# A recurrent kernel whose doubled cell moves from SBUF into the PSUM bank of its tanh

## The chip, the cores and the metric

The kernel runs on one core of one Trainium2 chip. A core has TensorE (PE, matmuls), VectorE (DVE), ScalarE (ACT), GpSimd (POOL) and SyncE (SP, which issues DMAs), each with a queue of its own that is worked off in order; they meet by semaphores. SBUF is the working memory, PSUM the memory of eight banks that matmuls write. The metric is the device time of one execution in microseconds, lower is better.

## The reference

The block has three layers over x of 16 batches x 1024 steps x 64 features: a token mixing (q, k, v, scores times a gamma matrix, output and PReLU), a recurrent autoencoder on its layernorm (LSTMs of 128 units), and a mixture of 8 experts, two chosen for each token, on the layernorm of the sum. The recurrent part is this, cut:

```
def step(carry, xw):
    h, c = carry
    z = xw + h @ U
    i, f, g, o = jnp.split(z, 4, axis=-1)
    i = jax.nn.sigmoid(i)
    f = jax.nn.sigmoid(f)
    g = jnp.tanh(g)
    o = jax.nn.sigmoid(o)
    c = f * c + i * g
    h = o * jnp.tanh(c)
    return ((h, c), h)
...
h_fwd = _lstm(x @ Wf + bf, Uf, reverse=False)
h_bwd = _lstm(x @ Wb + bb, Ub, reverse=True)
latent = jnp.concatenate([h_fwd, h_bwd], axis=-1)
rep = jnp.broadcast_to(latent[:, None, :], (x.shape[0], x.shape[1], 2 * H))
dec = _lstm(rep @ Wd + bd, Ud, return_sequences=True)
return dec @ Wo + bo
```

The two LSTMs of the encoder and the one of the decoder take 1024 steps each, one step after the other.

## The kernel before

Four stages run one behind the other: the setup of weights, the token mixing, the encoder and the decoder. The diff touches the last two.

A `Chain` is one LSTM: fwd and bwd in the encoder, dec in the decoder. Everything is held transposed, 128 units on the partitions and 16 batches in a row, so a step works on tiles of 128x16. A sigmoid is computed as a tanh of half the argument: sigmoid(z) = (tanh(z/2) + 1)/2. A step of a chain is:

- PE, `pe_gates`: 12 matmuls of 128x16 into the PSUM banks of the gates; eight with the high half of the hidden state (`h_hi`, f16; L740, weights `u_lo` and `u_hi`), four with its low half (`h_lo`; L743). The parts from x and the bias are already there (`fill`).
- ACT, `act_gates`: one tanh of the gates i, f, g (L751, 128x48, to `ifg_cell`), one of o (L753).
- DVE, `dve_terms` (L766): (tanh + 1) times its partner, for two pairs at once: i with g, f with the old cell, which lies in `ifg_cell[:, 3]`. `dve_sum` (L772) adds the two: twice the new cell, `twice_cell`, in SBUF.
- ACT, `act_cell` (L758): tanh of half of `twice_cell`, written to the start of a PSUM bank (6 for fwd, 7 for bwd, 3 for dec).
- DVE or ACT, the output gate from tanh_o: in the encoder ACT (L777), in the decoder DVE (L789).
- DVE, `dve_hidden`: the hidden state as f16, called hi below (L797), and again as f32, called h (L798); `dve_hidden_low` (L803): the difference, called lo. PE waits for hi and for lo.
- DVE, `dve_half_cell` (L783): half of `twice_cell` back to `ifg_cell[:, 3]`, for the next step's terms.

The order on each engine is written out by hand. In the encoder the two chains alternate, each pass of `for d in range(2)` being a half-step: DVE does hi and h of the other chain (`late`), terms of chain d, lo of the late chain, sum and halving of chain d. ACT does tanh of the cell, the gates and the output gate of one chain, then of the other. PE does one chain's gates and then filler matmuls (`pe_idle`, L731: products that nobody reads, which keep PE busy) or the next `fill`.

In the decoder there is one chain, and tiles of 32 steps (`BODY`): while it goes through 32 steps, the experts and layernorms of the 32 steps before run beside it, cut into pieces and tied to a step. On DVE such a piece stands either behind the halving and ahead of hi (`in_tanh`, while ACT computes the tanh of the cell) or behind lo (`in_gates`). PE has the expert matmuls and, in steps 2 to 18, 10 or 13 fillers.

An instruction that reads what its own engine has just written waits for that by a semaphore too: the sum for the terms, lo for h, the halving for the sum.

Of the kernel before, what the change touches and what calls it, by code (L numbers as in the profile page):

```python
# [7 lines left out]
ALU = mybir.AluOpType  # L8
ACT = mybir.ActivationFunctionType
# [692 lines left out]
class Chain:  # L702
# [5 lines left out]

    def __init__(self, sb, sem, d, name, cell_bank):
        self.d = d  # L710
        self.tanh_cell = cell_bank[:, 0:B]
        self.ifg_cell = sb(f"ifg_cell_{name}", [P, 4, B], F32)
        self.terms = sb(f"terms_{name}", [P, 2, B], F32)
        self.twice_cell, self.tanh_o, self.out_gate, self.h = (
            sb(f"{part}_{name}", [P, B], F32) for part in ("twice_cell", "tanh_o", "out_gate", "h"))
        (self.s_z_ifg, self.s_z_o, self.s_t_ifg, self.s_t_o, self.s_terms, self.s_out_gate, self.s_twice,
         self.s_cell, self.s_tanh_cell, self.s_hi, self.s_h, self.s_lo) = (sem(f"{s}_{name}") for s in (
             "z_ifg", "z_o", "t_ifg", "t_o", "terms", "out_gate", "twice", "cell", "tanh_cell", "hi", "h", "lo"))

    def start(self, nc, own):  # L720

        own.link(nc.vector.memset(self.twice_cell[:], 0.0))
        nc.vector.memset(self.ifg_cell[:, 3, :], 0.0).then_inc(self.s_cell, 1)


# [29 lines left out]

def act_cell(nc, act, c, n):
    act.wait_ge(c.s_twice, n + 1)
    nc.scalar.activation(c.tanh_cell, c.twice_cell[:], ACT.Tanh, scale=0.5).then_inc(c.s_tanh_cell, 1)  # L758


def dve_terms(nc, dve, c, n, own_cell=True):
# [7 lines left out]

def dve_sum(nc, dve, c, n):  # L770
    dve.wait_ge(c.s_terms, n + 1)
    nc.vector.tensor_tensor(c.twice_cell[:], c.terms[:, 0, :], c.terms[:, 1, :], ALU.add).then_inc(c.s_twice, 1)  # L772


def act_out_gate(nc, act, c, n, half_scale):
# [3 lines left out]


def dve_half_cell(nc, dve, c, sums):
    dve.wait_ge(c.s_twice, sums)
    nc.vector.tensor_scalar(c.ifg_cell[:, 3, :], c.twice_cell[:], 0.5, None, ALU.mult).then_inc(c.s_cell, 1)  # L783


def dve_rest(nc, dve, c, n, sums):

    dve.wait_ge(c.s_t_o, n + 1)
    nc.vector.tensor_scalar(c.out_gate[:], c.tanh_o[:], 1.0, 0.5 * X_SCALE, ALU.add, ALU.mult  # L789
                            ).then_inc(c.s_out_gate, 1)  # L790
    dve_half_cell(nc, dve, c, sums)


def dve_hidden(nc, dve, c, n, h_hi):
# [11 lines left out]
def encoder(nc, m):  # L806

    ctx, sb, sem = tools(nc)
    with ctx:
        ch = [Chain(sb, sem, d, name, m.bank[6 + d]) for d, name in enumerate(("fwd", "bwd"))]
        s_set = sem("encoder_state_set")
        hello = sb("encoder_hello", [P, 1], F32)
        half_scale = sb("encoder_half_scale", [P, 1], F32)
        s_half_scale = sem("half_scale_set")
        h = list(zip(m.enc_hi, m.enc_lo))


        banks = [[ifg_bank(m, 2 * d + p) for p in range(2)] for d in range(2)]
        o_banks = [o_bank(m, 4 + d) for d in range(2)]

        def at(d, step):

            q, s = divmod(step, STEPS)
            s = STEPS - 1 - s if d else s
            return banks[d][q % 2][:, s], o_banks[d][:, s]

        with nc.Block() as block:
            @block.tensor
            def _(pe):
                def fill(d, q, k):

                    g = SLOT_GATE[k]
                    z = banks[d][q % 2][:, :, k, :] if k < 3 else o_banks[d]
                    z = z.rearrange("p t b -> p b t")
                    x = m.xs[:, CHUNKS - 1 - q if d else q, :, :]

                    nc.tensor.matmul(z, m.w_hi[d][:, g, :], x,  # L841
                                     start=(k in (0, 3)), stop=False, skip_group_check=True)
                    nc.tensor.matmul(z, m.w_lo[d][:, g, :], x,  # L843
                                     start=False, stop=False, skip_group_check=True)
                    nc.tensor.matmul(z, m.lstm_bias[d][:, GATE_FROM[g], :], m.ones3[:].rearrange("p (b t) -> p b t", b=B),  # L845
                                     start=False, stop=False, skip_group_check=True)

                for d in range(2):
                    for k in range(4):
                        fill(d, 0, k)  # L850
                for step in range(T):
                    q, s = divmod(step, STEPS)
                    for d in range(2):
                        pe_gates(nc, pe, m, ch[d], step, h[d][0][:], h[d][1][:], *at(d, step))
                        spare = m.bank[2 * d + 1 - q % 2][:, HALF - P:]
                        if s in (1, 3, 5) and q + 1 < CHUNKS:
                            fill(d, q + 1, s // 2)
                            pe_idle(nc, m, spare, 2)
                        elif s != (STEPS - 1 if d else 0):
                            pe_idle(nc, m, spare, 5)  # L860
                        else:
                            pe_idle(nc, m, spare, 2)
                        if d == 1 and s == STEPS - 1 and q + 1 < CHUNKS:
                            pe.wait_ge(ch[0].s_t_o, step + 1)
                            fill(0, q + 1, 3)
                        if d == 0 and s == 0 and q > 0:
                            pe.wait_ge(ch[1].s_t_o, step)
                            fill(1, q, 3)

            @block.scalar  # L870
            def _(act):
                nc.scalar.activation(hello[:], m.ident[:, 0:1], ACT.Gelu)
                act.wait_ge(s_half_scale, 1)
                for n in range(T):
                    act_cell(nc, act, ch[1], n)
                    act_gates(nc, act, ch[0], n, *at(0, n))
                    act_out_gate(nc, act, ch[0], n, half_scale[:])
                    act_cell(nc, act, ch[0], n)
                    act_gates(nc, act, ch[1], n, *at(1, n))
                    act_out_gate(nc, act, ch[1], n, half_scale[:])  # L880
                act_cell(nc, act, ch[1], T)

            @block.vector
            def _(dve):
                own = Links(dve, s_set)
                nc.vector.memset(half_scale[:], 0.5 * X_SCALE).then_inc(s_half_scale, 1)
                for d in range(2):
                    ch[d].start(nc, own)
                own.link(nc.vector.memset(ch[1].out_gate[:], 0.0))
                nc.vector.memset(h[0][0][:], 0.0).then_inc(ch[0].s_hi, 1)  # L890
                nc.vector.memset(h[0][1][:], 0.0).then_inc(ch[0].s_lo, 1)
                nc.vector.memset(ch[1].h[:], 0.0).then_inc(ch[1].s_twice, 1)

                def hidden(late, n):
                    dve.wait_ge(ch[late].s_tanh_cell, n + 1)
                    dve_hidden(nc, dve, ch[late], n, h[late][0][:])

                for n in range(T):
                    for d in range(2):

                        late = 1 - d
                        hidden(late, n)
                        dve_terms(nc, dve, ch[d], n, own_cell=False)
                        dve_hidden_low(nc, dve, ch[late], n, h[late][0][:], h[late][1][:])
                        dve_sum(nc, dve, ch[d], n)
                        dve_half_cell(nc, dve, ch[d], n + 1 + d)
                hidden(1, T)
                dve_hidden_low(nc, dve, ch[1], T, h[1][0][:], h[1][1][:])

# [8 lines left out]
def decoder_and_experts(nc, m):  # L918
# [7 lines left out]
    with ctx:  # L926
# [74 lines left out]
        with nc.Block() as block:  # L1001
# [199 lines left out]
            def _(dve):  # L1201
# [139 lines left out]
                def body(i, tiles):  # L1341
                    tiles = [(j, start, Own(dve, s_own, DVE_OWN * j)) for j, start in tiles]
                    for step in range(BODY):
                        n = BODY * i + step
                        dve_terms(nc, dve, c, n)
                        dve_sum(nc, dve, c, n)
                        dve_rest(nc, dve, c, n, n + 1)
                        part(in_tanh, tiles, step)
                        dve.wait_ge(c.s_tanh_cell, n + 1)
                        dve.wait_ge(c.s_out_gate, n + 1)  # L1350
                        dve_hidden(nc, dve, c, n, h_at(ring_hi, n))
                        dve_hidden_low(nc, dve, c, n, h_at(ring_hi, n), h_at(ring_lo, n))
                        part(in_gates, tiles, step)

# [29 lines left out]
```

## Time and profile before

| what | us |
|---|---|
| median of 3 runs | 3970.09 |
| lowest and highest | 3967.66 and 3974.99 |
| the profiled execution | 3965.94 |
| its span, first to last instruction | 3964.1 |
| busy: PE, DVE, ACT | 3694.0, 3134.2, 2392.3 |

The profile is one execution, recorded by the hardware. A row of a timeline has the start and duration of an instruction, and an instruction can start while the one ahead of it is still ending. The distance between the starts of two instructions is what a step is made of. The grouped rows give a mean duration in ns for each line, operation and shape.

### The profile page before, as it was taken

How to read it: one execution, taken by the hardware profiler on the slowest of the kernel's cores; microseconds unless marked ns; L12 is line 12 of the kernel's file. 1: busy time of each engine (PE TensorE's matmuls, PEld its weight loads, DVE VectorE, ACT ScalarE, POOL GpSimd, SP SyncE). 2: the span in 40 equal slices, each digit the busy share in tenths (PEclk: the TensorE clock that was granted, in tenths of full speed). 3: DMA queues.
4: the chain of work that ended last, by engine and by line, in shares of the span. 5: the costliest groups of instructions: out<-in, count | busy, mean ns of one | idle time of the engine just before them, and what ended most of it. 6: DMA issues, size and time to landing. Idle time of an engine off the chain costs nothing. (4 is left out here: it accounts for less than half of the span.)

```text
span 3964.1 us, 155805 instructions
## 1 busy us (share of the span) xinstructions
PE 3694.0 (93%) x59839; PEld 2626.1 (66%) x59839; DVE 3134.2 (79%) x21227; ACT 2392.3 (60%) x11882; POOL 85.2 (2%) x129
## 2 busy tenths in 40 slices
PE   6899899999999999999999798989999999999898
PEld 3233688888888888888887556555555555555564
DVE  5888899999999999999998667766666666666675
ACT  3222699999999999999987334344334443344443
POOL 6100000000000000000000000000000000000000
PEclk8999999999999999999999899999999999999999
DMA  3010000000000000000000000000000000000000
GB/s 90 20 24 20 7 3 3 3 3 3 3 3 3 3 3 3 3 3 3 3 3 4 5 6 7 8 6 7 6 8 8 6 6 7 7 7 7 6 7 7
DMA packets 49554, 33.73 MB, mean 9 GB/s; under 512 B 37661, under 2 KB 46877, under 8 KB 48806
## 3 DMA queue, kind: packets, MB, share of 16 engines
q1 hardware_dynamic: 48806, 23.77, 2.3%
q8 instruction: 468, 7.67, 0.8%
q14 instruction: 280, 2.29, 0.2%
HBM read 15.37 MB, written 8.39 MB: 6 GB/s over the span
## 5 line engine op out<-in xcount | busy, mean ns | idle before, releaser
L731 PE MATMUL bank<-xs,ident 128*128 128x128 f16 x13490 | 1209.0, 221 | 0.0
L731 PEld LDWEIGHTS bank<-xs,ident 128*128 128x128 f16 x13490 | 882.4, 102 | 60.5 <-issue 38.2
L751 ACT ACTIVATE ifg_cell_dec<-bank 128x48 f32<-128x48 f32 x1024 | 215.1, 210 | 664.7 <-PE bank L743 664.7
L766 DVE SCALAR_TENSOR_TENSOR terms_dec<-ifg_cell_dec 128x32 f32<-128x32 f32 x1024 | 196.5, 192 | 422.6 <-ACT ifg_cell_dec L751 411.7
L743 PE MATMUL bank<-enc_lo,u_hi 128*128 128x16 f16 x8192 | 529.2, 173 | 0.3 <-DVE enc_lo L803 0.3
L740 PE MATMUL bank<-enc_hi,u_lo 128*128 128x16 f16 x8192 | 527.0, 172 | 0.0
L740 PE MATMUL bank<-enc_hi,u_hi 128*128 128x16 f16 x8192 | 500.3, 169 | 0.0
L740 PEld LDWEIGHTS bank<-ring_hi,u_lo 128*128 128x128 f16 x4096 | 175.5, 97 | 485.1 <-DVE ring_hi L797 465.4
L740 PEld LDWEIGHTS bank<-enc_hi,u_lo 128*128 128x128 f16 x8192 | 338.8, 96 | 205.5 <-DVE enc_hi L797 171.4
L758 ACT ACTIVATE bank<-twice_cell_dec 128x16 f32<-128x16 f32 x1024 | 191.8, 187 | 401.9 <-DVE twice_cell_dec L772 401.9
L740 PE MATMUL bank<-ring_hi,u_lo 128*128 128x16 f16 x4096 | 264.2, 173 | 181.6 <-DVE ring_hi L797 148.4
L743 PEld LDWEIGHTS bank<-enc_lo,u_hi 128*128 128x128 f16 x8192 | 338.5, 96 | 67.5 <-DVE enc_lo L803 0.4
L740 PEld LDWEIGHTS bank<-enc_hi,u_hi 128*128 128x128 f16 x8192 | 349.6, 95 | 0.0
L777 ACT ACTIVATE out_gate_fwd<-tanh_o_fwd,encoder_half_scale 128x16 f32<-128x16 f32 x1024 | 315.2, 308 | 33.5
L777 ACT ACTIVATE out_gate_bwd<-tanh_o_bwd,encoder_half_scale 128x16 f32<-128x16 f32 x1024 | 314.9, 308 | 33.6
L843 PE MATMUL bank<-xs,w_lo 128*128 128x128 f16 x1024 | 322.4, 315 | 0.0
L845 PE MATMUL bank<-ones,bias 128*128 128x128 bf16 x1024 | 322.3, 315 | 0.0
L841 PE MATMUL bank<-xs,w_hi 128*128 128x128 f16 x1024 | 277.3, 271 | 1.4 <-PEq L432 1.4
L743 PE MATMUL bank<-ring_lo,u_hi 128*128 128x16 f16 x4096 | 263.2, 172 | 0.9 <-DVE ring_lo L803 0.9
L1112 PE MATMUL bank<-hid,w 128*64 128x512 f32 x448 | 258.1, 660 | 0.0
L740 PE MATMUL bank<-ring_hi,u_hi 128*128 128x16 f16 x4096 | 250.6, 169 | 0.0
L758 ACT ACTIVATE bank<-twice_cell_bwd 128x16 f32<-128x16 f32 x1025 | 192.0, 187 | 53.9
(268 smaller groups left out, 7900.4 us busy)
## 6 DMA issues: line engine op xcount, KB each, us to landing
g_rows<-tok_d_gamma_batched_dram SPq DMA_DIRECT2D x8, 512.0 KB, 6.5
x_rows<-in_x_dram SPq DMA_DIRECT2D x16, 256.0 KB, 3.1
kept_h<-tok_ln_h SPq DMA_DIRECT2D x32, 128.0 KB, 2.1
res<-kept_h SPq DMA_DIRECT2D x32, 128.0 KB
out_dram<-sums SPq DMA_DIRECT2D x32, 128.0 KB
raw_wd<-in_L_attn_Wd_dram SPq DMA_DIRECT2D x2, 256.0 KB
raw_experts<-in_L_ffn_W_dram SPq DMA_DIRECT2D x2, 256.0 KB
raw_u<-in_L_attn_Uf_dram SPq DMA_DIRECT2D x1, 256.0 KB
```

The lines of the kernel that those rows point to most:

```text
L731: nc.tensor.matmul(spare, m.ident16[:], m.xs[:, 0, :, :].rearrange("p b t -> p (b t)"), start=False, stop=True, skip_group_check=True)
L740: nc.tensor.matmul(z[k], w[:, g, :], h_hi, start=False, stop=False, skip_group_check=True)
L743: last = nc.tensor.matmul(z[k], m.u_hi[c.d][:, g, :], h_lo, start=False, stop=True, skip_group_check=True)
L751: nc.scalar.activation(c.ifg_cell[:, 0:3, :], ifg, ACT.Tanh, scale=1.0 / Z_SCALE).then_inc(c.s_t_ifg, 1)
L758: nc.scalar.activation(c.tanh_cell, c.twice_cell[:], ACT.Tanh, scale=0.5).then_inc(c.s_tanh_cell, 1)
L766: nc.vector.scalar_tensor_tensor(c.terms[:], c.ifg_cell[:, 0:2, :], 1.0, c.ifg_cell[:, 2:4, :], ALU.add, ALU.mult).then_inc(c.s_terms, 1)
L777: nc.scalar.activation(c.out_gate[:], c.tanh_o[:], ACT.Identity, scale=0.5 * X_SCALE, bias=half_scale).then_inc(c.s_out_gate, 1)
L841: nc.tensor.matmul(z, m.w_hi[d][:, g, :], x, start=(k in (0, 3)), stop=False, skip_group_check=True)
L843: nc.tensor.matmul(z, m.w_lo[d][:, g, :], x, start=False, stop=False, skip_group_check=True)
L845: nc.tensor.matmul(z, m.lstm_bias[d][:, GATE_FROM[g], :], m.ones3[:].rearrange("p (b t) -> p b t", b=B), start=False, stop=False, skip_gro ...
L1112: mm(y_bank[0:D, :], m.w2[:, e, :], hid[:, e % 2, :], start=False, stop=False, skip_group_check=True)
```

## The change

`twice_cell` no longer has an SBUF tile of its own. It is the second block of 16 columns in the chain's cell bank in PSUM, beside the tanh, so DVE's sum writes PSUM, and ACT's tanh and DVE's halving read it there. The halving, which stood beside the tanh, is moved behind it: in the decoder to between h and lo, in the encoder to half a step later, where it halves the late chain's cell. The terms of the encoder need it, and a wait for `s_cell` is added ahead of hi.

```diff
-        self.tanh_cell = cell_bank[:, 0:B]
+        self.tanh_cell, self.twice_cell = cell_bank[:, 0:B], cell_bank[:, B:2 * B]
...
 def dve_sum(nc, dve, c, n):
     dve.wait_ge(c.s_terms, n + 1)
-    nc.vector.tensor_tensor(c.twice_cell[:], c.terms[:, 0, :], c.terms[:, 1, :], ALU.add).then_inc(c.s_twice, 1)
+    nc.vector.tensor_tensor(c.twice_cell, c.terms[:, 0, :], c.terms[:, 1, :], ALU.add).then_inc(c.s_twice, 1)
...
 def dve_half_cell(nc, dve, c, sums):
     dve.wait_ge(c.s_twice, sums)
-    nc.vector.tensor_scalar(c.ifg_cell[:, 3, :], c.twice_cell[:], 0.5, None, ALU.mult).then_inc(c.s_cell, 1)
...
-def dve_rest(nc, dve, c, n, sums):
+    nc.vector.tensor_scalar(c.ifg_cell[:, 3, :], c.twice_cell, 0.5, None, ALU.mult).then_inc(c.s_cell, 1)
...
+def dve_out_gate(nc, dve, c, n):
...
-    dve_half_cell(nc, dve, c, sums)
...
                         late = 1 - d
+                        dve.wait_ge(ch[d].s_cell, n + 1 + d)
                         hidden(late, n)
                         dve_terms(nc, dve, ch[d], n, own_cell=False)
                         dve_hidden_low(nc, dve, ch[late], n, h[late][0][:], h[late][1][:])
                         dve_sum(nc, dve, ch[d], n)
-                        dve_half_cell(nc, dve, ch[d], n + 1 + d)
+                        dve_half_cell(nc, dve, ch[late], n + 1)
...
                         dve_sum(nc, dve, c, n)
-                        dve_rest(nc, dve, c, n, n + 1)
+                        dve_out_gate(nc, dve, c, n)
                         part(in_tanh, tiles, step)
                         dve.wait_ge(c.s_tanh_cell, n + 1)
                         dve.wait_ge(c.s_out_gate, n + 1)
                         dve_hidden(nc, dve, c, n, h_at(ring_hi, n))
+                        dve_half_cell(nc, dve, c, n + 1)
                         dve_hidden_low(nc, dve, c, n, h_at(ring_hi, n), h_at(ring_lo, n))
```

DVE's queue in the encoder, one half-step of the kernel before; in brackets the semaphores that an instruction waits for (`twice` is set by the sum, `cell` by the halving, `t_ifg` by ACT's tanh of the gates):

```order
L797 TENSOR_TENSOR enc_hi<-out_gate_bwd,bank 128x16 [waits tanh_cell_bwd]
L798 TENSOR_TENSOR h_bwd<-out_gate_bwd,bank 128x16
L766 SCALAR_TENSOR_TENSOR terms_fwd<-ifg_cell_fwd 128x32 [waits t_ifg_fwd]
L803 TENSOR_TENSOR enc_lo<-h_bwd,enc_hi 128x16 [waits h_bwd]
L772 TENSOR_TENSOR twice_cell_fwd<-terms_fwd 128x16 [waits terms_fwd]
L783 TENSOR_SCALAR ifg_cell_fwd<-twice_cell_fwd 128x16 [waits twice_fwd]
```

The same half-step of the changed kernel:

```order
L797 TENSOR_TENSOR enc_hi<-out_gate_bwd,bank 128x16 [waits tanh_cell_bwd,cell_fwd]
L798 TENSOR_TENSOR h_bwd<-out_gate_bwd,bank 128x16
L766 SCALAR_TENSOR_TENSOR terms_fwd<-ifg_cell_fwd 128x32 [waits t_ifg_fwd]
L803 TENSOR_TENSOR enc_lo<-h_bwd,enc_hi 128x16 [waits h_bwd]
L772 TENSOR_TENSOR bank<-terms_fwd 128x16 [waits terms_fwd]
L784 TENSOR_SCALAR ifg_cell_bwd<-bank 128x16 [waits twice_bwd]
```

The halving at the end is now that of the other chain, whose sum was half a step before, and hi has a second wait.

DVE's queue in the decoder, one step of the kernel before, from terms to lo:

```order
L766 SCALAR_TENSOR_TENSOR terms_dec<-ifg_cell_dec 128x32 [waits cell_dec,t_ifg_dec]
L772 TENSOR_TENSOR twice_cell_dec<-terms_dec 128x16 [waits terms_dec]
L789 TENSOR_SCALAR out_gate_dec<-tanh_o_dec 128x16 [waits t_o_dec]
L783 TENSOR_SCALAR ifg_cell_dec<-twice_cell_dec 128x16 [waits twice_dec]
L797 TENSOR_TENSOR ring_hi<-out_gate_dec,bank 128x16 [waits out_gate_dec,tanh_cell_dec]
L798 TENSOR_TENSOR h_dec<-out_gate_dec,bank 128x16
L803 TENSOR_TENSOR ring_lo<-h_dec,ring_hi 128x16 [waits h_dec]
```

And of the changed kernel:

```order
L772 TENSOR_TENSOR bank<-terms_dec 128x16 [waits terms_dec]
L790 TENSOR_SCALAR out_gate_dec<-tanh_o_dec 128x16 [waits t_o_dec]
L797 TENSOR_TENSOR ring_hi<-out_gate_dec,bank 128x16 [waits out_gate_dec,tanh_cell_dec]
L798 TENSOR_TENSOR h_dec<-out_gate_dec,bank 128x16
L784 TENSOR_SCALAR ifg_cell_dec<-bank 128x16 [waits twice_dec]
L803 TENSOR_TENSOR ring_lo<-h_dec,ring_hi 128x16 [waits h_dec]
```

The halving has moved from ahead of hi to between h and lo. The order on ACT and PE is the same as before.

## Rows read from the trace of the kernel before

**Rows 1.** Busy time by stretch, encoder and decoder; last columns granted clock, DMA share, GB/s.

```profile
426.00:2159.00 1733.00, 1732.72 (x34795) 1459.98 (x34792) 1571.27 (x12279) 1560.28 (x8187) 0.00 (x0) 1.00 0.01 3
2166.00:3926.00 1760.00, 1577.71 (x22856) 1021.90 (x22856) 1214.97 (x8273) 699.24 (x3470) 0.00 (x0) 0.97 0.03 7
```

**Rows 2.** Timeline of an encoder half-step: start us, duration us, engine, line, operation, out<-in.

```profile
1502.22 0.21 ACT L751 ACTIVATE ifg_cell_bwd<-bank 128x48 f32<-128x48 f32 x1
...
1502.28 0.17 DVE L797 TENSOR_TENSOR enc_hi<-out_gate_fwd,bank 128x16 f16<-128x16 f32 x1
...
1502.36 0.16 DVE L798 TENSOR_TENSOR h_fwd<-out_gate_fwd,bank 128x16 f32<-128x16 f32 x1
1502.47 0.19 DVE L766 SCALAR_TENSOR_TENSOR terms_bwd<-ifg_cell_bwd 128x32 f32<-128x32 f32 x1
...
1502.58 0.17 DVE L803 TENSOR_TENSOR enc_lo<-h_fwd,enc_hi 128x16 f16<-128x16 f32 x1
...
1502.80 0.26 PE L743 MATMUL bank<-enc_lo,u_hi 128*128 128x16 f16 x4
...
1503.07 0.21 ACT L751 ACTIVATE ifg_cell_fwd<-bank 128x48 f32<-128x48 f32 x1
```

**Rows 3.** Timeline of a plain decoder step.

```profile
3074.99 0.17 DVE L772 TENSOR_TENSOR twice_cell_dec<-terms_dec 128x16 f32<-128x16 f32 x1
...
3075.20 0.19 ACT L758 ACTIVATE bank<-twice_cell_dec 128x16 f32<-128x16 f32 x1 [0.39 <-DVE twice_cell_dec L772]
...
3075.42 0.17 DVE L797 TENSOR_TENSOR ring_hi<-out_gate_dec,bank 128x16 f16<-128x16 f32 x1
3075.51 0.16 DVE L798 TENSOR_TENSOR h_dec<-out_gate_dec,bank 128x16 f32<-128x16 f32 x1
...
3075.70 0.17 DVE L803 TENSOR_TENSOR ring_lo<-h_dec,ring_hi 128x16 f16<-128x16 f32 x1
...
3075.94 0.26 PE L743 MATMUL bank<-ring_lo,u_hi 128*128 128x16 f16 x4
...
3076.21 0.21 ACT L751 ACTIVATE ifg_cell_dec<-bank 128x48 f32<-128x48 f32 x1 [0.82 <-PE bank L743]
...
3076.45 0.19 DVE L766 SCALAR_TENSOR_TENSOR terms_dec<-ifg_cell_dec 128x32 f32<-128x32 f32 x1 [0.57 <-ACT ifg_cell_dec L751]
...
3076.67 0.17 DVE L772 TENSOR_TENSOR twice_cell_dec<-terms_dec 128x16 f32<-128x16 f32 x1
```

**Rows 4.** Timeline of a decoder step that TensorE holds.

```profile
3051.33 0.17 DVE L797 TENSOR_TENSOR ring_hi<-out_gate_dec,bank 128x16 f16<-128x16 f32 x1
...
3051.36 0.90 PE L731 MATMUL bank<-xs,ident 128*128 128x128 f16 x13
...
3052.09 0.25 PE L740 MATMUL bank<-ring_hi,u_lo 128*128 128x16 f16 x4
```

**Rows 5.** Groups by line and form, ScalarE, decoder: count | busy us, mean ns | idle.

```profile
L751 ACT ACTIVATE ifg_cell_dec<-bank 128x48 f32<-128x48 f32 x1023 | 214.9, 210 | 659.7 <-PE bank L743 659.7
L758 ACT ACTIVATE bank<-twice_cell_dec 128x16 f32<-128x16 f32 x1023 | 191.6, 187 | 401.5 <-DVE twice_cell_dec L772 401.5
```

**Rows 6.** Groups by line and form, whole span.

```profile
L623 DVE TENSOR_TENSOR gated<-bank,gammaT 128x512 f32<-128x512 f32 x256 | 172.4, 685 | 6.0 <-PE bank L474 5.1
...
L1170 ACT COPY xn<-bank 128x512 f16<-128x512 f16 x32 | 18.5, 579 | 1.2 <-PE bank L1068 1.2
...
L1175 ACT COPY ff_h_kept<-ff_h 128x256 f32<-128x256 f32 x32 | 12.4, 388 | 0.0
L635 DVE TENSOR_SCALAR neg<-bank,a_col 128x512 f32<-128x512 f32 x16 | 11.9, 741 | 2.9 <-PE bank L510 2.9
```

**Rows 7.** Groups by line and form, ScalarE, the setup.

```profile
L278 ACT COPY raw_wvo<-bank 128x64 f32<-128x64 f32 x1 | 0.2, 212 | 0.5 <-PE bank L262 0.5
```

**Rows 8.** Groups by line and form, VectorE, start of the decoder.

```profile
L1212 DVE TENSOR_TENSOR given_left<-given,given_parts 128x64 f32<-128x64 f32 x1 | 0.2, 224 | 0.0
L1209 DVE COPY given<-bank 128x64 f32<-128x64 f32 x1 | 0.2, 223 | 0.3 <-PE bank L1135 0.3
```

More of the change, by code:

```diff
@@ L710, in __init__ @@
         self.d = d
-        self.tanh_cell = cell_bank[:, 0:B]
+        self.tanh_cell, self.twice_cell = cell_bank[:, 0:B], cell_bank[:, B:2 * B]
         self.ifg_cell = sb(f"ifg_cell_{name}", [P, 4, B], F32)
         self.terms = sb(f"terms_{name}", [P, 2, B], F32)
-        self.twice_cell, self.tanh_o, self.out_gate, self.h = (
-            sb(f"{part}_{name}", [P, B], F32) for part in ("twice_cell", "tanh_o", "out_gate", "h"))
+        self.tanh_o, self.out_gate, self.h = (
+            sb(f"{part}_{name}", [P, B], F32) for part in ("tanh_o", "out_gate", "h"))
         (self.s_z_ifg, self.s_z_o, self.s_t_ifg, self.s_t_o, self.s_terms, self.s_out_gate, self.s_twice,
@@ L720, in start @@
     def start(self, nc, own):
-        own.link(nc.vector.memset(self.twice_cell[:], 0.0))
+        own.link(nc.vector.memset(self.twice_cell, 0.0))
         nc.vector.memset(self.ifg_cell[:, 3, :], 0.0).then_inc(self.s_cell, 1)
@@ L757, in act_cell @@
     act.wait_ge(c.s_twice, n + 1)
-    nc.scalar.activation(c.tanh_cell, c.twice_cell[:], ACT.Tanh, scale=0.5).then_inc(c.s_tanh_cell, 1)
+    nc.scalar.activation(c.tanh_cell, c.twice_cell, ACT.Tanh, scale=0.5).then_inc(c.s_tanh_cell, 1)
 def dve_terms(nc, dve, c, n, own_cell=True):
```

## The prediction

> **What bounds the kernel now.** I read the views in this order: busy time by stretch, a timeline of a piece of each recurrence, then the grouped rows for the price of each operation.
>
> The stretches [rows 1] say that two recurrences fill the span: the encoder from 426 to 2159 us and the decoder from 2166 to 3926 us. TensorE is nearly always busy in the first and 90% busy in the second, but much of that is filler matmuls that keep its clock up, so its share says nothing yet. The timelines say what a step waits for.
>
> In the **encoder** two chains, fwd and bwd, take turns on every engine, one half-step each. Follow the second chain of [rows 2]: tanh of bwd's three gates on ACT starts at 1502.22, DVE's terms of bwd at 1502.47, then DVE's low half of the *other* chain's hidden state at 1502.58, the matmuls with it (L743) at 1502.80, and the tanh of fwd's gates at 1503.07, which is where bwd's stood 0.85 us before. Each of these starts as soon as the one ahead allows it: ACT's 0.21 us and 0.03 to 0.04 of hand-over, DVE's next slot (0.11), and twice PE's latency (0.22 and 0.27, the second the same as in the decoder, where ACT sits idle before it). So this loop, gates, terms, low half, matmul, gates, closes in 0.25+0.11+0.22+0.27 = 0.85 us, the length of a half-step. **The doubled cell and its tanh are not in it.** They are in a second loop (terms, sum, tanh of the cell, hi, h, and then the next terms on DVE's queue), and that one has a little air: h to the next terms is 0.11 (1502.36 to 1502.47), where two neighbours with nothing to wait for stand 0.08 to 0.09 apart (hi to h). The air is the difference, some 20 ns; with times printed to 10 ns it may be 10 or 30.
>
> In the **decoder** there is one chain, and [rows 3] shows it as one string: sum 3074.99, tanh of the cell 3075.20, hi 3075.42, h 3075.51, lo 3075.70, PE 3075.94, gates 3076.21, terms 3076.45, sum again 3076.67. A plain step is 1.68 us, and no wait in it is for anything else. Exceptions are steps in which PE comes late: in [rows 4] hi is there at 3051.33, but PE takes it at 3052.09, 0.76 later, where lo to its matmul is 0.24 in the plain step, because 13 filler matmuls, begun at 3051.36 behind large expert matmuls, stand ahead of it. This is step 2 of a tile of 32; steps 5 and 6 are held by PE too, by less. In such a step PE's own work sets the length, and an earlier hi gains nothing. So 29 of 32 steps, 928 of 1024, follow the chain. The decoder's mean granted clock is 0.97 [rows 1], which is 6% of the time at the lower level of 1.2 GHz instead of 2.4; some of those steps are held by PE too, and I take all of them away: 928 x 0.94 = **872 steps**.
>
> **The change part by part.**
>
> *ACT's tanh of the cell reads PSUM instead of SBUF* (destination PSUM as before). Now it takes 187 ns [rows 5]. The row that reads PSUM, L751, takes 210 for 48 elements [rows 5]. For the slope, two copies out of PSUM: 579 for 512 elements [rows 6] and 212 for 64 [rows 7], (579-212)/448 = 0.82 ns for an element. L751 with 16 would then take 210 - 32x0.82 = 184, but that one writes SBUF. What the source alone does is shown by the copy that reads SBUF and writes SBUF, 388 for 256 [rows 6], against the copy out of PSUM at the same size, 212 + 192x0.82 = 369: 19 ns less from PSUM. So the saving is between 3 (187 to 184, if the destination brings nothing) and 19. I take 16, near the copies, because they differ in the source and in nothing else that counts, while the 3 leaves PSUM as a destination at no gain. No row has a PSUM source dearer on ACT, so I exclude a loss on this term; the copies were not all waiting for the same thing, which may be worth some 10 ns either way, so its upper end is 30.
>
> *DVE's sum writes PSUM instead of SBUF.* No DVE instruction of this trace writes PSUM. The nearest rows are reads: a copy out of PSUM, 223 ns for 64 elements, against a tensor_tensor within SBUF of the same size, 224 [rows 8]. By them a PSUM operand costs DVE nothing, and I take 0. A gain is not excluded (ACT's rows show that a PSUM port can be the quicker one): bound it at -10, half of ACT's 19. The far end upward is a DVE row with a PSUM operand that is dear for its size: L635, 741 for 512 elements, against L623, 685, with PSUM among its sources too [rows 6]. 56 ns is what such a surcharge could be, though L635 also reads a scalar by pointer, which is the likelier reason for it.
>
> The Trainium skill, page "VectorE: DVE Perf Modes", section "The TRN2 errata — SBUF-src ops pay a fixed extra latency per instruction", gives fixed costs by source: VectorE 58 cycles from SBUF and 120 from PSUM, ScalarE 224 and 172. At its clocks (0.96 and 1.2 GHz) that is 65 ns more for a VectorE operation on PSUM and 43 less for a ScalarE one; taken for the sum's destination too, of which the table does not speak, the chain would lose 22 ns in a step, an estimate of 19 us slower over 872 steps. The trace does not bear out its VectorE half for reads (223 against 224, where it would say some 65 more), and its ScalarE half by less than half the size (19 for 43).
>
> *The halving moves.* In the **decoder** it stood after out_gate, waiting for the sum's end, and began together with the tanh (3075.20 is its start too): beside the tanh, costing nothing. Now it stands between h and lo. DVE starts neighbours 0.09 apart, so h at 0, the halving at 0.09, and lo may start at 0.18. But lo waits for h anyway and starts 0.19 after it [rows 3]. So the halving fits in a gap that is already there, with 10 to 20 ns over: 0. If that cover is gone (a slot of 0.11, as terms to lo in the encoder takes with 32 elements), lo comes up to 20 ns later, 872 x 20 = 17 us, all of the gain. The halved cell is needed by the next terms, 0.94 after h: no wait. The router and layernorm operations that DVE does beside the tanh only get an earlier slot.
>
> In the **encoder** the halving of chain d moved from behind its own sum to behind the other chain's, half a step later, where it has no semaphore left to wait for; DVE then waits for the tanh in any case. The new wait ahead of hi, for the halving issued a half-step before, has been met long before the tanh is done. What is queued behind it are hi, h, terms and lo, and PE waits for hi and lo; it costs them nothing, since in the decoder hi has two waits already and follows the start of its tanh by 0.22, 0.19 of which is the tanh itself [rows 3]. 0 for both. And the shorter tanh: 0, because the other loop holds the half-step; what comes late next is nothing new, the gates loop was last already.
>
> **The sum.** 872 x 16 ns = 14.0 us. Against the profiled execution's own 3965.9 us that is 3951.9; the median of the runs shown, 3970.1, lies 4.2 above it, so by the median **3956 us**, 0.35% less.
>
> **The rivals.**
>
> *No difference.* The tanh saves only a few ns (the L751 reading), or DVE's write or a late lo takes back what it saves. With a net of 3 ns: 872 x 3 = 2.6 us, 3967. Everything from 9 ns saved to 9 ns lost is in this case.
>
> *Slower: DVE's write to PSUM is the dear one.* The place is the sum, in the decoder on the chain at full price, in the encoder on the loop that has 20 ns of air. With the far bound, 56 - 16 = 40 ns net: decoder 872 x 40 = 35 us; encoder 2048 half-steps x (40-20) = 41 us; together 76, 4046. It decides from 25 ns for the write (16 saved and 9 more); from 36 the encoder joins, and each ns then costs more than three times as much (872 and 2048 instead of 872). For it: no row shows a DVE write to PSUM. Against it: reads at 223 and 224.
>
> *The encoder gains as well.* If the air in its second loop were none, and the gates loop were only its echo, each half-step would shorten too: 2048 x 16 = 33 us more, 3923. Against it: the 0.11 after h where 0.08 to 0.09 would do.
>
> **How the numbers follow.** Forecast (9 to 30 ns saved in a step) 0.60; no difference 0.22; slower by DVE's write 0.13; the encoder too 0.05. About 0.2%, 8 us, is what a measurement of this kernel can tell from no change; that is 9 ns in a step. So faster 0.65, same 0.22, slower 0.13. The range holds the forecast with 30 ns saved (872 x 30 = 26, 3944, and 2 for the spread of runs) and, on the other side, the no-difference case to 7 ns lost (6 us, 3976): 3942 to 3976. Outside are the slower rival and the encoder's gain, 0.18.
>
> **What the changed kernel's profile would show.** The tanh of the cell at 171 ns or so in all three chains; the sum still at 174 to 175; a plain decoder step of 1.67 instead of 1.68 us, with h to lo still 0.20; the encoder's half-step still 0.85, with h to the next terms grown by what the tanh lost. The prediction is wrong if the sum's row grows, if lo stands over 0.20 behind h in the decoder, or if the encoder's stretch changes its length.

## The result, and the profile after

The changed kernel takes 4054.99 us (median of 4 runs, 4040.5 to 4056.6) against 3971.11; the ratio is 1.020, with an interval of 1.019 to 1.021. It is slower by 84 us, and the prediction, 3956 with a range to 3976, was wrong in its sign.

The page of the profiled execution, its span, busy times and granted clock in 40 slices:

```profile
span 4054.8 us, 157853 instructions
...
PE 3752.5 (93%) x59839; PEld 2632.6 (65%) x59839; DVE 2812.9 (69%) x21227; ACT 2362.2 (58%) x11882; POOL 85.2 (2%) x129
...
PEclk8999999999999999999999888999999999999998
```

Busy time in the two recurrences; columns as in [rows 1], with the same places in the program at either end:

```profile
428.00:2239.00 1811.00, 1765.44 (x34778) 1461.88 (x34775) 1332.24 (x12274) 1554.53 (x8184) 0.00 (x0) 1.00 0.01 3
2246.00:4016.00 1770.00, 1597.99 (x22855) 1023.57 (x22856) 1132.91 (x8276) 674.22 (x3469) 0.00 (x0) 0.95 0.02 7
```

The encoder went from 1733 to 1811 us, the decoder from 1760 to 1770 [rows 1]. So 79 of the 91 us between the two profiled executions (4056.58 and 3965.94) lie in the encoder, where the prediction put nothing, and the decoder, where the gain was to be, is longer too, at a mean clock of 0.95 instead of 0.97.

A piece of the encoder's timeline, DVE and ACT, answering to [rows 2]:

```profile
1501.04 0.18 DVE L772 TENSOR_TENSOR bank<-terms_bwd 128x16 f32<-128x16 f32 x1
1501.13 0.17 DVE L784 TENSOR_SCALAR ifg_cell_fwd<-bank 128x16 f32<-128x16 f32 x1
...
1501.26 0.17 ACT L758 ACTIVATE bank<-bank 128x16 f32<-128x16 f32 x1
...
1501.53 0.17 DVE L797 TENSOR_TENSOR enc_hi<-out_gate_bwd,bank 128x16 f16<-128x16 f32 x1 [0.23 <-ACT bank L758]
...
1501.61 0.17 DVE L798 TENSOR_TENSOR h_bwd<-out_gate_bwd,bank 128x16 f32<-128x16 f32 x1
1501.69 0.18 DVE L766 SCALAR_TENSOR_TENSOR terms_fwd<-ifg_cell_fwd 128x32 f32<-128x32 f32 x1
...
1501.91 0.18 DVE L772 TENSOR_TENSOR bank<-terms_fwd 128x16 f32<-128x16 f32 x1
```

From sum (1501.04) to sum (1501.91) a half-step is 0.87 us instead of 0.85. The tanh takes 0.17 and ends at 1501.43, but hi starts at 1501.53: **0.27 behind the tanh's start**, of which 0.10 stand behind its end. From the next row on all is quick, h to terms 0.08. The loop that had 20 ns of air is now the one that closes last. The view of waits for DVE in the encoder puts it in one line (us in total, times, longest); no row of it stood there before:

```profile
DVE enc_hi L797 <- ACT bank L758: 468.9, 2043, 0.6
```

And DVE's sequencer has an instruction that it didn't have, one ahead of each hi:

```profile
L895 DVEq EVENT_SEMAPHORE  x1920: 21/21/21, 500.4 to 2199.2; - x192
```

A plain decoder step, answering to [rows 3]:

```profile
3101.01 0.18 DVE L772 TENSOR_TENSOR bank<-terms_dec 128x16 f32<-128x16 f32 x1
...
3101.23 0.17 ACT L758 ACTIVATE bank<-bank 128x16 f32<-128x16 f32 x1 [0.40 <-DVE bank L772]
3101.43 0.17 DVE L797 TENSOR_TENSOR ring_hi<-out_gate_dec,bank 128x16 f16<-128x16 f32 x1 [0.16 <-ACT bank L758]
3101.52 0.16 DVE L798 TENSOR_TENSOR h_dec<-out_gate_dec,bank 128x16 f32<-128x16 f32 x1
3101.60 0.17 DVE L784 TENSOR_SCALAR ifg_cell_dec<-bank 128x16 f32<-128x16 f32 x1
...
3101.72 0.17 DVE L803 TENSOR_TENSOR ring_lo<-h_dec,ring_hi 128x16 f16<-128x16 f32 x1
...
3102.69 0.18 DVE L772 TENSOR_TENSOR bank<-terms_dec 128x16 f32<-128x16 f32 x1
```

Here the tanh's start to hi is 0.20, and a step 1.68 (its median over all plain steps is 1.675 us after and 1.684 before). Grouped rows of the decoder, answering to [rows 5]:

```profile
L772 DVE TENSOR_TENSOR bank<-terms_dec 128x16 f32<-128x16 f32 x983 | 179.5, 183 | 33.5
...
L758 ACT ACTIVATE bank<-bank 128x16 f32<-128x16 f32 x983 | 165.1, 168 | 394.6 <-DVE bank L772 394.6
...
L784 DVE TENSOR_SCALAR ifg_cell_dec<-bank 128x16 f32<-128x16 f32 x983 | 164.4, 167 | 0.6
```

In the kernel before, the sum and the halving were these:

```profile
L772 DVE TENSOR_TENSOR twice_cell_dec<-terms_dec 128x16 f32<-128x16 f32 x1022 | 178.2, 174 | 34.8
L783 DVE TENSOR_SCALAR ifg_cell_dec<-twice_cell_dec 128x16 f32<-128x16 f32 x1022 | 178.0, 174 | 0.0
```

The sum's write to PSUM costs 183 ns instead of 174, the tanh's read from there 168 instead of 187.

### The profile page after: what moved, and what is told of

The parts are those of the page before. It is cut to its first block and busy times, and to the rows that moved or that the text cites. A ratio compares the mean times of both kernels' runs of the same rounds, so it can differ in the third digit from the quotient of the medians.

```text
span 4054.8 us, 157853 instructions
## 1 busy us (share of the span) xinstructions
PE 3752.5 (93%) x59839; PEld 2632.6 (65%) x59839; DVE 2812.9 (69%) x21227; ACT 2362.2 (58%) x11882; POOL 85.2 (2%) x129
## 5 line engine op out<-in xcount | busy, mean ns | idle before, releaser
L758 ACT ACTIVATE bank<-bank 128x16 f32<-128x16 f32 x3073 | 516.3, 168 | 567.1 <-DVE bank L772 438.4
L797 DVE TENSOR_TENSOR enc_hi<-out_gate_fwd,bank 128x16 f16<-128x16 f32 x1024 | 175.1, 171 | 237.3 <-ACT bank L758 237.0
L797 DVE TENSOR_TENSOR enc_hi<-out_gate_bwd,bank 128x16 f16<-128x16 f32 x1025 | 175.2, 171 | 233.4 <-ACT bank L758 233.4
L797 DVE TENSOR_TENSOR ring_hi<-out_gate_dec,bank 128x16 f16<-128x16 f32 x1024 | 174.5, 170 | 147.7 <-ACT bank L758 133.2
L1113 PE MATMUL bank<-hid,w 128*64 128x512 f32 x448 | 274.8, 699 | 0.0
```

The source lines that it names most:

```text
L758: nc.scalar.activation(c.tanh_cell, c.twice_cell, ACT.Tanh, scale=0.5).then_inc(c.s_tanh_cell, 1)
L797: tt(h_hi, c.out_gate[:], c.tanh_cell, ALU.mult).then_inc(c.s_hi, 1)
L1113: mm(y_bank[0:D, :], m.w2[:, e, :], hid[:, e % 2, :], start=False, stop=False, skip_group_check=True)
```

## The experiments

The two queues in the section on the change already hold the clue, in the order of the brackets. Hi waits for `out_gate_dec,tanh_cell_dec` in the decoder and for `tanh_cell_bwd,cell_fwd` in the encoder of the changed kernel. In all traces of this kernel an instruction carries one wait of its own; a second one becomes a separate wait instruction ahead of it (L895 above), and it is the first in the brackets that is separate. The compiler puts the wait that the source names *last* there. In the decoder the separate one is the output gate's, met long before; in the encoder it is the tanh's, which is met last. **Theory W**: what follows a separate wait that has to wait starts some 70 ns later than an instruction that waits itself. The rivals: **P**, work in PSUM delays hi, and **M**, the halving that now stands just ahead of hi delays it.

All numbers in one table (medians and ratios to the kernel before of the same chip; the encoder's length from the profiled execution, first to last terms of the fwd chain; the clock is the mean over the runs):

| kernel | us | ratio, interval | clock | encoder us | plain decoder step, ns |
|---|---|---|---|---|---|
| before | 3966 to 3971 | | 0.977 to 0.979 | 1732.4 | 1684 |
| changed | 4054.99 | 1.020, 1.019 to 1.021 | 0.969 | 1811.2 | 1675 |
| e1, waits swapped | 3992.26 | 1.006, 1.005 to 1.008 | 0.969 | 1746.4 | 1675 |
| e2, extra wait | 4072.28 | 1.027, 1.025 to 1.028 | 0.976 | 1838.0 | 1685 |
| e3, moved, in SBUF | 3977.91 | 1.003, 1.002 to 1.004 | 0.983 | 1750.9 | 1687 |
| e4, decoder's waits | 4046.83 | 1.021, 1.020 to 1.023 | 0.969 | 1734.8 | 1755 |
| e5, wait on terms | 3972.93 | 1.0018, 1.0007 to 1.0029 | 0.979 | 1742.5 | 1685 |
| e6, wait on h | 3967.57 | 0.9997, 0.9983 to 1.0011 | 0.974 | 1733.4 | 1676 |
| e7, decoder only | 3972.20 | 1.0009, 0.9996 to 1.0022 | 0.971 | 1735.5 | 1676 |
| e8, e6 and filler | 3946.89 | 0.9948, 0.9935 to 0.9961 | 0.984 | 1733.2 | 1675 |
| e9, filler alone | 3954.24 | 0.9967, 0.9954 to 0.998 | 0.985 | 1732.9 | 1685 |

**e1**, the changed kernel with the two waits in the other order:

```diff
-                        dve.wait_ge(ch[d].s_cell, n + 1 + d)
-                        hidden(late, n)
+                        dve.wait_ge(ch[late].s_tanh_cell, n + 1)
+                        dve.wait_ge(ch[d].s_cell, n + 1 + d)
+                        dve_hidden(nc, dve, ch[late], n, h[late][0][:])
```

> The changed kernel with one edit: in the encoder the wait for the tanh of the cell stands ahead of the wait for the halving in the source, instead of behind it, so that the instruction's own wait becomes that for the tanh and the separate wait instruction is the one for the halving. Theory W (the separate wait instruction waits for the tanh, and what follows such a wait starts some 68 ns late): hi follows the start of the tanh by 0.20 us in the encoder instead of 0.27, the half-step goes from 0.875 back to 0.847 us, the encoder from 1811 to about 1733 us, and the decoder keeps its 9 ns a step; time about 3963 us, up to 3975 with clock dips in the decoder. Rival P (DVE's or ACT's work in PSUM delays hi) and rival M (the halving issued just ahead of hi delays it): nothing changes, 0.27 and about 4055 us.

Timeline of its encoder, the tanh of the cell and hi behind it:

```profile
602.29 0.17 ACT L758 ACTIVATE bank<-bank 128x16 f32<-128x16 f32 x1
...
602.49 0.17 DVE L797 TENSOR_TENSOR enc_hi<-out_gate_bwd,bank 128x16 f16<-128x16 f32 x1 [0.16 <-ACT bank L758]
```

0.20, as expected (the median of all is 200 ns, where the changed kernel has 270), and the half-step is 0.847 again. The encoder lost 65 of its 79 extra us by the order of two source lines. But it stayed 14 us above the kernel before, and the whole 26, which W alone doesn't explain; e5 to e9 are about that rest.

**e2**, the kernel before with nothing but a second wait in the changed kernel's place:

```diff
                         late = 1 - d
+                        dve.wait_ge(ch[d].s_cell, n + 1)
                         hidden(late, n)
```

> The kernel before (doubled cell in SBUF, halving behind its own sum) with only a second wait ahead of the encoder's hi, for a halving that is long done, put in the source where the change puts it. Theory W: hi follows the start of its tanh by 0.285 instead of 0.22 us, the half-step becomes 0.88 to 0.89 us, and the time 4045 to 4060 us, as slow as the changed kernel although no operand and no operation moved. Rivals P and M: within 0.2% of the kernel before, 3971 us.

Timeline of its encoder, tanh, hi, and the next half-step's hi:

```profile
1501.18 0.19 ACT L758 ACTIVATE bank<-twice_cell_bwd 128x16 f32<-128x16 f32 x1
...
1501.46 0.17 DVE L797 TENSOR_TENSOR enc_hi<-out_gate_bwd,bank 128x16 f16<-128x16 f32 x1
...
1502.35 0.17 DVE L797 TENSOR_TENSOR enc_hi<-out_gate_fwd,bank 128x16 f16<-128x16 f32 x1
```

0.28 from the tanh's start to hi (median 289 ns, 219 before) and 0.89 for a half-step. The half-step grows by 41 ns where hi comes 70 later, so the loop had 29 ns of air. With the doubled cell in SBUF and nothing moved, the kernel is even slower than the changed one, whose quicker tanh, less what its sum costs more, takes some 10 ns off each half-step of the same loop. P and M are out as causes of the large part.

**e3**, the changed kernel with the doubled cell in SBUF, waits as in e1:

```diff
-        self.tanh_cell, self.twice_cell = cell_bank[:, 0:B], cell_bank[:, B:2 * B]
+        self.tanh_cell, self.twice_cell = cell_bank[:, 0:B], sb(f"twice_cell_{name}", [P, B], F32)[:]
```

> The changed kernel with the doubled cell back in SBUF and the waits of the encoder's hi swapped as in e1: the move of the halving alone. Theory W: the move costs nothing, 3971 us within 0.2%, encoder's half-step 0.847, plain decoder step 1.684 us with the tanh at 187 ns and the sum at 175. Rival M: 4040 us or more. Rival P says the same as W here, and is told apart by e1.

The decoder is as expected, 1687 ns a step: the halving between h and lo costs 2 or 3 ns. The encoder is 18 us longer than before, where e1's is 14. So the rest is not PSUM's.

**e4**, the kernel before with the waits ahead of the *decoder's* hi swapped:

```diff
-                        dve.wait_ge(c.s_tanh_cell, n + 1)
-                        dve.wait_ge(c.s_out_gate, n + 1)
+                        dve.wait_ge(c.s_out_gate, n + 1)
+                        dve.wait_ge(c.s_tanh_cell, n + 1)
```

> The kernel before with one edit in the decoder: the waits for the output gate and for the tanh ahead of hi swapped in the source, so that there too the separate wait is the one for the tanh. Theory W, in a place that the change does not touch: hi follows the tanh's start by 0.285 to 0.29 instead of 0.22 us, the plain step grows from 1.684 to about 1.75 us, and over some 870 steps the time by 58 us, to about 4029. If the order of two waits is of no account (P, M): 3971.

Timeline of its decoder, a sum, the tanh, hi, and the next sum:

```profile
3001.66 0.17 DVE L772 TENSOR_TENSOR twice_cell_dec<-terms_dec 128x16 f32<-128x16 f32 x1
...
3001.87 0.19 ACT L758 ACTIVATE bank<-twice_cell_dec 128x16 f32<-128x16 f32 x1 [0.39 <-DVE twice_cell_dec L772]
...
3002.16 0.17 DVE L797 TENSOR_TENSOR ring_hi<-out_gate_dec,bank 128x16 f16<-128x16 f32 x1
...
3003.41 0.18 DVE L772 TENSOR_TENSOR twice_cell_dec<-terms_dec 128x16 f32<-128x16 f32 x1
```

0.29 instead of 0.22, 1.75 instead of 1.68 us a step, and 81 us more in the whole, of which 77 are in the decoder. The expected 58 was too small, since the mean clock fell as well and more steps than 870 followed the chain. W holds in a place that the change doesn't touch.

**What e1 left over.** In the traces of the changed kernel, e1, e2 and e3 most encoder half-steps are alike, and four to six in 128 are longer, because one instruction in them starts up to 0.35 us late. Count DVE's records (its lines in the trace, waits included) from the encoder's first terms, in blocks of 128: nearly all of the late ones are number 75 of a block, whatever instruction that is. The encoder of the kernel before has six records in a half-step, these have seven. **e5** gives the kernel before a seventh, away from hi, and moves nothing:

```diff
-                        dve_terms(nc, dve, ch[d], n, own_cell=False)
+                        dve_terms(nc, dve, ch[d], n)
```

> The kernel before with one separate wait more in each encoder half-step, ahead of terms, for a halving that is long done (terms' own wait stays that for the gates). Nothing is moved, nothing is in PSUM, and hi's wait is as before, but DVE's stream has seven instructions for a half-step instead of six, as in the changed kernel. Theory F (with the seventh instruction a hold of up to 0.3 us at every 128th DVE instruction, seen in the changed kernel, e1, e2 and e3 and never in the encoder of the kernel before, comes into view): median half-step 0.847, some 80 longer ones, the encoder 14 us longer, time about 0.35% above the kernel before. Rival M2 (the halving moved next to hi opens the loop to that hold): no long half-steps, same time as before.

Timeline of DVE, h to terms in a usual half-step and in a long one:

```profile
449.99 0.17 DVE L798 TENSOR_TENSOR h_bwd<-out_gate_bwd,bank 128x16 f32<-128x16 f32 x1
450.10 0.19 DVE L766 SCALAR_TENSOR_TENSOR terms_fwd<-ifg_cell_fwd 128x32 f32<-128x32 f32 x1
...
450.85 0.17 DVE L798 TENSOR_TENSOR h_fwd<-out_gate_fwd,bank 128x16 f32<-128x16 f32 x1
451.21 0.19 DVE L766 SCALAR_TENSOR_TENSOR terms_bwd<-ifg_cell_bwd 128x32 f32<-128x32 f32 x1 [0.20 <-issue]
```

0.11 in the first, 0.36 in the second. Its encoder has 48 half-steps with an instruction held by 0.08 us or more, all at number 75 of a block, and that of the kernel before has none; the encoder is 10 us longer, and the time 0.18% above (interval 0.07 to 0.29). So the seventh instruction is enough (F), and the halving's move is not needed. The size was expected somewhat larger (80 long half-steps and 14 us). Of e3's 18 us 12 are in 64 long half-steps and some 6 in the others, which are 3 ns longer in the mean; where those 3 ns come from was not tested.

**e6** takes the seventh away again: the wait goes on h, which has none of its own.

```diff
-                        dve.wait_ge(ch[d].s_cell, n + 1 + d)
-                        hidden(late, n)
+                        dve.wait_ge(ch[late].s_tanh_cell, n + 1)
+                        nc.vector.tensor_tensor(h[late][0][:], ch[late].out_gate[:], ch[late].tanh_cell, ALU.mult
+                                                ).then_inc(ch[late].s_hi, 1)
+                        dve.wait_ge(ch[d].s_cell, n + 1 + d)
+                        nc.vector.tensor_tensor(ch[late].h[:], ch[late].out_gate[:], ch[late].tanh_cell, ALU.mult
+                                                ).then_inc(ch[late].s_h, 1)
```

> The changed kernel with the encoder's wait for the halving put on h, which has no wait of its own, instead of ahead of hi: no separate wait instruction, six DVE instructions in a half-step, hi waits for the tanh alone. Theory W with F: hi 0.20 us behind its tanh's start, half-step 0.847 throughout, the encoder back at 1733 us, the plain decoder step 1.675; time 8 us below the kernel before if the decoder's mean clock is as before, 3957 to 3960, and up to 10 above it if the clock is lower as it was in e1. If the work in PSUM itself cost the encoder anything, the encoder stays above 1735 us.

Busy time of its encoder and decoder:

```profile
427.00:2160.00 1733.00, 1732.87 (x34773) 1458.78 (x34774) 1411.26 (x12273) 1542.79 (x8183) 0.00 (x0) 1.00 0.01 3
2167.00:3930.00 1763.00, 1589.13 (x22855) 1022.77 (x22856) 1133.55 (x8276) 674.13 (x3468) 0.00 (x0) 0.95 0.02 7
```

The encoder is back at 1733 us: with the wait placed well, the change costs it nothing, as predicted, and gives it nothing. The decoder's step is 1676 ns, and still the decoder is not shorter, at a mean clock of 0.95. **e7** has the change in the decoder alone:

```diff
-                        dve.wait_ge(ch[d].s_cell, n + 1 + d)
...
-                        dve_half_cell(nc, dve, ch[late], n + 1)
+                        dve_half_cell(nc, dve, ch[d], n + 1 + d)
...
+        if not twice_in_psum:
+            self.twice_cell = sb(f"twice_cell_{name}", [P, B], F32)[:]
```

> The change in the decoder alone, the encoder word for word as before. The sum there takes 183 instead of 175 ns and the tanh 168 instead of 187, so the plain step is 9 ns shorter: by that sum 8 us below the kernel before. Theory C (the shorter step lowers the mean granted clock in the decoder, which gives the gain back): mean clock 0.967 to 0.973 against 0.98 before, and the time within 0.3% of before, above it rather than below. Rival: the lower clock of e1 came from something else in it, the clock here is 0.98 and the time 8 us below.

No difference from the kernel before, with a mean clock of 0.971 over 12 runs against 0.977 over 29. Within one kernel time goes with the clock: over the 29 runs of before a line fits with 19 us for 0.01 of clock (correlation 0.99), and over e6's 12 with 18. Read off such lines at a clock of 0.979, before is at 3965.5, e6 at 3958.0, e7 at 3957.1 (its own line, 21 us for 0.01, carried beyond its highest clock of 0.975). So the 8 us that the shorter step was worth are there, and the clock takes them back.

Where does it fall? Let a step of a tile go from its terms to the next terms, and the first be number 0. In the decoder of the kernel before the clock drops 13 times, in the changed kernel's 22 times, and all but two of each begin in the same step, number 21, behind its hi, with which TensorE begins the gates of step 22 (the expectation of e8 calls the place step 22). Behind such a drop step 22 takes 2.32 us instead of 1.68; there are 10 such steps before and 21 after, and 11 x 0.64 = 7 us, nearly the gain. A tile of e6, steps 20 and 21, in whose last 0.9 us the drop has begun, and the 17 us behind:

```profile
2863.40:2866.70 3.30, 2.56 (x33) 1.50 (x32) 1.80 (x14) 1.43 (x8) 0.00 (x0) 0.87 0.02 5
2866.70:2883.70 17.00, 17.00 (x126) 5.78 (x126) 7.32 (x56) 5.80 (x28) 0.00 (x0) 0.52 0.01 1
```

TensorE worked 2.56 of 3.30 us in steps 20 and 21. In step 20 alone it is idle for a third, more than in any other step of a tile (0.24 is the next): step 20 has no filler, since they end with step 18, and little expert work. Right behind them the clock is 0.52 for 17 us, nearly all of it at the 1.2 GHz level; this is one of the long drops, and most end within 4 us. That idle time can't be the whole cause, though. Steps 7 and 8 of the same tile, steps 9 and 10, and the 15 us up to step 20:

```profile
2841.60:2844.90 3.30, 2.53 (x53) 2.14 (x51) 2.56 (x21) 0.85 (x7) 0.00 (x0) 1.00 0.00 0
2844.90:2848.20 3.30, 2.53 (x52) 2.07 (x49) 2.50 (x16) 1.18 (x8) 0.00 (x0) 1.00 0.00 0
2848.20:2863.40 15.20, 14.21 (x242) 10.83 (x241) 10.69 (x80) 6.05 (x33) 0.00 (x0) 1.00 0.04 12
```

TensorE works no more there, 2.53 of 3.30 us, and in no tile behind the first of before, changed, e6 or e7 does a drop begin in steps 7 to 19. Whether filling step 20 helps is a question of its own. **e8** puts 8 fillers into step 20 of e6, **e9** into step 20 of the kernel before:

```diff
                             pe_idle(nc, m, m.bank[1 - q % 2][:, HALF - P:], 10 if s % 2 else 13)
+                        elif step == 20:
+                            pe_idle(nc, m, m.bank[1 - q % 2][:, HALF - P:], 8)
```

> e6 (the changed kernel with the wait on h) with 8 more filler matmuls in step 20 of each decoder tile. In the profiles all clock dips of the decoder but the first begin in step 22 of a tile, and TensorE is idle for a third of step 20 and 12% of step 21, the most in a tile. Theory C2 (the idle ahead of step 22 brings the dips, and more of them with the shorter step): fewer dips, mean clock 0.98 or more instead of 0.9735, and the full gain of the shorter step comes through: 3950 to 3958 us, 0.3% to 0.5% below the kernel before. Rival: the dips come from something else, the clock stays at 0.97, and the time at 3968.

> The kernel before with the same 8 fillers in step 20 and nothing else. Theory C2: the clock rises from 0.978 to 0.98 or more and the time falls by up to 10 us, so that e8 and e9 differ by the 8 us of the shorter decoder step. Rival: time and clock as before, 3968 us and 0.978.

The same two stretches of a tile of e8:

```profile
2853.20:2856.50 3.30, 3.11 (x41) 1.81 (x40) 1.79 (x14) 1.45 (x8) 0.00 (x0) 1.00 0.00 0
2856.50:2873.50 17.00, 15.33 (x161) 6.80 (x160) 9.13 (x70) 7.45 (x36) 0.00 (x0) 1.00 0.01 2
```

3.11 of 3.30 us of work, and a clock of 1.00 in the 17 us behind. In e8's whole decoder no drop begins at the old place any more; besides the first, in tile 0, there are 8 short ones, all in step 6. Its encoder, and its decoder up to 3900 us:

```profile
427.00:2160.00 1733.00, 1732.72 (x34783) 1458.94 (x34780) 1409.67 (x12269) 1543.03 (x8181) 0.00 (x0) 1.00 0.01 3
2167.00:3900.00 1733.00, 1572.30 (x23065) 1040.17 (x23062) 1128.50 (x8249) 671.76 (x3458) 0.00 (x0) 0.98 0.03 7
```

The clock is 0.98 in the decoder and 0.984 in the mean of the runs, 0.985 in e9, and the times follow: e9 3954.2, e8 3946.9. Both beat the kernel before, e8 by 0.52% (interval 0.39 to 0.65), and both by a little more than was expected of them. With nearly the same clock in both, **7.4 us stand between them: the 8 that the shorter decoder step was worth.**

## Why the prediction was wrong, point by point

*What bounds the kernel.* Right: e6's encoder has a tanh 19 ns shorter and the length of before, and the plain decoder step shows every ns. Steps 2, 5 and 6 of a tile, which the prediction took out, are as long in the changed kernel as before. The air in the encoder's second loop is 29 ns (e2), at the upper end of the 10 to 30 given.

*The tanh from PSUM, 16 ns.* 19 measured, exactly what the copies gave.

*DVE's write to PSUM, 0.* 8 to 9 measured (183 for 174 or 175). This term was mis-sized: the only rows were of reads, and those cost nothing. 19 less, 8 to 9 more and 2 or 3 for the moved halving leave 9 ns less in a plain step (1675 for 1684), where the sum had 16. The Trainium skill, page "VectorE: DVE Perf Modes", section "The TRN2 errata — SBUF-src ops pay a fixed extra latency per instruction", gives fixed costs by source, from which the estimate is 43 ns less for ScalarE reading PSUM and 65 more for VectorE. The runs bear out the sign on ScalarE, with 19, and nothing on VectorE: the halving between h and lo takes 167 ns from PSUM (changed kernel) and 168 from SBUF (e3). Of writes the table doesn't speak.

*The halving moves, 0.* Right within 3 ns in the decoder: lo stands 0.20 behind h (3101.52 and 3101.72), and e3's step is 2 or 3 ns longer. Right in the encoder too, where e6 has the moved halving and the length of before.

*The new wait ahead of hi, 0.* **This step failed, and it is what made the kernel slower: 79 us in the encoder by its two effects, the order of the waits and the extra record, where e6, with the same wait on h, has neither and is level with the kernel before.** The prediction looked at when the semaphore is set ("met long before"), and at the decoder, where hi has two waits and follows its tanh by 0.22. What counts is which of two waits the compiler makes the separate instruction. The order in the brackets of the queues on record gives it, to a reader who knows that the first in them is the separate one. The price: 70 ns between tanh and hi (289 for 219 in e2 and e4, 270 for 200 in the changed kernel and e1). Less the 19 of the quicker tanh, plus the 8 of the sum, less some 30 of air, that is the 28 ns of the half-step's median (0.847 to 0.875), 2048 x 28 = 57 us. In the same breath the text said that the halving was issued a half-step before. It is issued just before the hi that waits for it, though it too is done by then.

*Instructions counted only by the waits they bring.* The separate wait also made seven records of six in a half-step, and the holds at number 75 of each 128 cost the rest of the encoder's 79 us: its 84 long half-steps have 20 us more than the median. No term stood for that.

*The sum.* 872 x 9 = 8 us instead of 14; runs at like clock show 8 (e6 and e7) and 7.4 (e8 less e9). The term was right in kind and 6 too large, and then the clock took it: the mean clock was assumed to stay as it was. So the forecast gain would not have come without the wait's cost either: e6 is at 0.9997 of the kernel before.

*The rivals.* Of the slower rival the number nearly came true (4046), but not its mechanism: DVE's write cost 9 ns and not 56, the decoder's chain got shorter and not longer, and the encoder was held by a wait instruction. That near hit was luck. Two of the signs that the prediction named for being wrong did show: the sum's row grew and the encoder's stretch changed its length.

## What to carry to other kernels

Of two waits in front of an instruction on the critical path, the one met last must be the instruction's own, and not a separate one: look up which is which in the compiled order, or place the second wait on a neighbour that has none. Count a wait in a tight loop as an instruction, even when it is met long before: e5's cost 10 us. And compare kernels with fillers for TensorE at like granted clock: a shorter step on another engine can lower it and hide its own gain, and fillers in the step ahead of the drops may be worth more than the change (13 us alone, against 7 to 8).

## What the runs showed of the hardware

- An instruction behind a separate wait on DVE that has to wait starts 66 ns behind the start of that wait's record (median in the changed kernel's encoder, e2's encoder and e4's decoder), and 70 ns later than if it waited itself (289 for 219 ns behind the tanh's start in e2 and e4, 270 for 200 in the changed kernel against e1).
- Where the encoder's loop has seven DVE records to a half-step, the instruction at number 75 of a block of 128 is held by up to 0.35 us, in 48 (e5) to 96 (changed kernel) of 112 blocks; where it has six, never. The decoder of the kernel before has such holds too (five of h behind hi, by 0.24 us). That this is the fetching of the next block of instructions is only likely: among the 8 KB instruction fetches of e1's encoder is a series that comes every 15.6 us, which is 128 records. In the encoder of the kernel before there is one every 18.1 us, 128 records as well, and nothing is held; why six records hide it was not found out.
- Two copies, one from PSUM and one from SBUF, told what ACT saves by reading PSUM to the ns (19); DVE's write to PSUM costs 8 to 9 ns more than to SBUF at 128x16, while its read from there was no dearer (the halving, 167 ns from PSUM in the changed kernel, 168 from SBUF at the same place in e3).
- TensorE's clock fell behind two steps in which it worked 2.56 of 3.30 us, and not behind the same steps with 3.11 of 3.30 (e8 and e9). It did not fall behind steps 7 to 10, where it worked 2.53 of 3.30, so the share alone doesn't decide it, and what else does stays open. Open too is why a step shorter by 9 ns brings more drops with the same fillers (13 and 22 of them); e3, whose step is 3 ns longer than before, had 3.
